# Graph message passing on one core: four groups of three edge tiles in place of six pairs, and normalisation written back into the gather buffer

## What is computed

```python
h = jnp.maximum(_layernorm(x, axis=-1), 0.0)
x_i, x_j = h[src], h[dst]
x_ij = jnp.concatenate([x_i, x_j], axis=1)
m_ij = jax.nn.relu(x_ij @ W.T + b)
out = jax.ops.segment_sum(m_ij, src, num_segments=50000)
return x + out
```

## Time and profile before

| | |
|---|---|
| median of three runs | 763.47 us (762.25 to 765.0) |
| the profiled execution | 760.78 us, span 759.1 us |
| TensorE | 717.7 us busy, 95% of the span |
| VectorE | 590.6 us, 78% |
| ScalarE | 470.0 us, 62% |
| GpSimd | 365.3 us, 48% |
| mean DMA rate | 241 GB/s |

### The profile page before, as it was taken

One profiled execution on the slowest core, in us unless ns is written; L12 is line 12 of the kernel. 1 busy time (PEld: TensorE's weight loads), 2 busy tenths in 40 slices (PEclk: granted clock), 3 DMA queues, 4 the chain that ended last, 5 costly groups with the idle time before them and its releaser, 6 DMA issues.

```text
span 759.1 us, 13504 instructions
## 1 busy us (share of the span) xinstructions
PE 717.7 (95%) x3490; PEld 589.7 (78%) x3490; DVE 590.6 (78%) x1972; ACT 470.0 (62%) x892; POOL 365.3 (48%) x305
## 2 busy tenths in 40 slices
PE   7699999999999999999999999999999999999940
PEld 6578888888888888888888888888888888888830
DVE  4588788788888888878888888878878878878620
ACT  5466667567577576576576576566666666666510
POOL 7632232232232232322167777777776777644433
PEclk9899999999999999999999999999999999999985
DMA  8999999999999999999868787878878787856564
GB/s 276 360 381 365 364 351 374 349 374 362 370 364 359 372 369 351 372 363 344 314 117 142 159 133 147 152 151 133 167 129 152 143 135 143 148 65 78 63 82 55
DMA packets 35750, 182.72 MB, mean 241 GB/s; under 512 B 7306, under 2 KB 7502, under 8 KB 33720
## 3 DMA queue, kind: packets, MB, share of 16 engines
q0 software_dynamic: 29792, 77.00, 49.5%
q1 hardware_dynamic: 5552, 105.39, 36.1%
q10 hardware_dynamic: 392, 0.20, 0.1%
HBM read 156.96 MB, written 128.61 MB: 376 GB/s over the span
## 4 chain that ended last, share of the span: by engine, by line
PE 78%; DMA 9%; issue 5%; POOL 5%; DVE 1%; ACT 0%; SPq 0%; POOLq 0%; DVEq 0%; ACTq 0%
PE z_ps L514 20%; PE z_ps L515 20%; PE z_ps L516 20%; PE ht_ps L498 10%; DMA out<-ring,add_i 6%; POOL out L203 4%; DMA xg<-x,dst_i 3%; POOL xg L187 2%; PE agg_ps L526 1%; PE agg_ps L532 1%; PE agg_ps L527 1%; PE agg_ps L528 1%; PE agg_ps L531 1%; PE agg_ps L529 1%; DMA src_i<-src_cols 0%
## 5 line engine op out<-in xcount | busy, mean ns | idle before, releaser
L514 PE MATMUL z_ps<-w_hi,ht_hi 128*128 128x512 f32 x784 | 319.2, 407 | 1.9 <-DVE w_lo L355 1.1
L515 PE MATMUL z_ps<-w_lo,ht_hi 128*128 128x512 f32 x784 | 310.5, 396 | 0.0
L516 PE MATMUL z_ps<-w_hi,ht_lo 128*128 128x512 f32 x784 | 310.3, 396 | 0.0
L398 ACT CAST ht_hi<-ht_ps 128x512 fp32r<-128x512 f32 x196 | 105.9, 590 | 231.8 <-PE ht_ps L498 231.5
L187 POOL DMA_INDIRECT xg<-x,src_i x98 | 103.1, 1052 | 237.8 <-ACT h L407 223.0
L203 POOL DMA_INDIRECT out<-ring,add_i x98 | 157.7, 1609 | 117.9 <-DMA out<-ring,add_i 82.4
L516 PEld LDWEIGHTS z_ps<-w_hi,ht_lo 128*128 128x128 f32 x784 | 147.6, 188 | 36.0
L514 PEld LDWEIGHTS z_ps<-w_hi,ht_hi 128*128 128x128 f32 x784 | 147.9, 189 | 34.0 <-issue 1.5
L515 PEld LDWEIGHTS z_ps<-w_lo,ht_hi 128*128 128x128 f32 x784 | 148.1, 189 | 31.8
L241 DVE BATCH_NORM_STATS2 stats<-xg 128x6 f32<-128x512 f32 x196 | 125.6, 682 | 15.7 <-DMA xg<-x,dst_i 11.0
L414 ACT ACTIVATE h<-h,rstd 128x512 f32<-128x512 f32 x196 | 131.7, 727 | 2.3 <-DVE rstd L268 2.3
(11 more groups left out here) (45 smaller groups left out, 434.1 us busy)
## 6 DMA issues: line engine op xcount, KB each, us to landing
out<-x SPq DMA_DIRECT2D x125, 800.0 KB, 8.5
ring<-w_t SPq DMA_DIRECT2D x4, 512.0 KB, 4.6
xg<-x,src_i POOLq DMA_INDIRECT x98, 9.5
xg<-x,dst_i POOLq DMA_INDIRECT x98, 23.8
out<-ring,add_i POOLq DMA_INDIRECT x98, 5.0
row_lanes<-src_rows ACTq DMA_DIRECT2D x49, 4.0 KB
out<-x SPq DMA_DIRECT2D x1, 512.0 KB, 9.0
bias_bc<-bias SPq DMA_DIRECT2D x1, 256.0 KB, 8.1
```

The source lines that it names most:

```text
L398: nc.scalar.copy(ht_hi[:, b, s, :], ht_ps[b][s][:, :]).then_inc(hi_ready, 1)
L514: nc.tensor.matmul(z_ps[b][:, :], hi, w_hi[:, c, :], start=(c == 0), stop=False)
L515: nc.tensor.matmul(z_ps[b][:, :], hi, w_lo[:, c, :], start=False, stop=False)
L516: last = nc.tensor.matmul(z_ps[b][:, :], lo, w_hi[:, c, :], start=False, stop=(c == K - 1))
```

## The change

Tiles 0 to 83 stay in 42 pairs. Tiles 84 to 95 form four groups of three in place of six pairs, and tiles 96 and 97 stay a pair. In a group of three the comparison has up to 384 columns, and the first tile's sum has six matmuls, the second's four and the third's two. There are still two accumulators for sums, so the third sum uses the first one's again: it is made one step later, after the first has been stored. ScalarE stores the first two sums at the start of its step and the third after `centre`. The spare region has 384 rows in place of 256, and SyncE fills one that much larger. Each group waits for the group before it to land.

Both passes of the normalisation write into the slot of `xg` that they read, and `h` is gone. So TensorE's transposes read the slot, and the gather of tile t waits for them (`transposed`) and no longer for `centred`. ScalarE's `centre` loses its wait for `transposed`. TensorE's loop has eight steps in its body in place of two, since the slot is named in the instruction, and the last steps are written out from tile 83 on.

```diff
+    TRIPLES = 4
+    FIRST3 = TILES - 2 - 3 * TRIPLES
+    GROUPS = ([(f, 2) for f in range(0, FIRST3, 2)] + [(f, 3) for f in range(FIRST3, TILES - 2, 3)]
+              + [(TILES - 2, 2)])
...
             def gather(t):
                 b = t % XS
                 if t >= XS:
-                    pool.wait_ge(centred, SIDES * (t - XS + 1))
+                    pool.wait_ge(transposed, SIDES * (t - XS + 1))
...
-            def add(pair):
+            def add(group):
+                first, size = GROUPS[group]
...
-                    pool.wait_ge(scattered, 32 * pair)
-                pool.wait_ge(add_ready, 2 * pair + 2)
-                for t in (2 * pair, 2 * pair + 1):
+                    pool.wait_ge(scattered, 16 * first)
+                pool.wait_ge(add_ready, first + size)
+                for t in range(first, first + size):
...
-            sp.dma_start(out[N:N + 2 * P, :], x[0:2 * P, :]).then_inc(spare_filled, 16)
+            sp.dma_start(out[N:N + 3 * P, :], x[0:3 * P, :]).then_inc(spare_filled, 16)
...
-                if not (isinstance(t, int) and t < 2):
-                    act.wait_ge(transposed, SIDES * (t - 1))
                 for s in range(SIDES):
-                    nc.scalar.activation(h[:, b, s, :], xg[:, m, s, :], ACT.Relu, bias=neg_mean[:, b, s:s + 1]
+                    nc.scalar.activation(xg[:, m, s, :], xg[:, m, s, :], ACT.Relu, bias=neg_mean[:, b, s:s + 1]
...
-                    nc.scalar.activation(h[:, b, s, :], h[:, b, s, :], ACT.Copy, scale=rstd[:, b, s:s + 1]
+                    nc.scalar.activation(xg[:, m, s, :], xg[:, m, s, :], ACT.Copy, scale=rstd[:, b, s:s + 1]
...
+            def first_sums_of_triple(t):
+                pe.wait_ge(same_ready, t + 3)
+                pe.wait_ge(ring_filled, t)
+                pe.wait_ge(mlo_ready, t + 3)
+                sum_of(0, ((0, 0), (1, 1), (3, 2)))
+                sum_of(1, ((2, 1), (4, 2)))
+            def last_sum_of_triple(t):
+                pe.wait_ge(ring_filled, t + 1)
+                sum_of(0, ((5, 2),))
...
-            with pe.Fori(3, TILES - 4, 2) as s:
-                for d in range(2):
-                    step(s + d, (3 + d) % 2)
+            with pe.Fori(3, 3 + XS * (rounds - 1) + 1, XS) as s:
+                for d in range(XS):
+                    step(s + d, (3 + d) % XS, pair=d % 2 == 1)
```

More of the change, by code:

```diff
@@ L141, in gnn_message_passing_kernel, with place, sums_before @@
         ring_filled = sem("ring_filled")
+        def place(t, b):
+            if not isinstance(t, int) or t < FIRST3 or t >= TILES - 2:
+                return b, t - b, 2
+            pos = (t - FIRST3) % 3
+            return pos, t - pos, 3
+        def sums_before(t, b):
+            pos, first, size = place(t, b)
+            if isinstance(t, int) and first == 0:
+                return 0
+            last = place(first - 1, 1)[2] if isinstance(t, int) else 2
+            return first - last + min(pos + 1, last)
         block = ctx.enter_context(nc.Block())
@@ L225, in _ @@
             for t in range(FIRST_ADD, TILES):
-                while added < min((t - FIRST_ADD + 1) * 7 // 8, (t - 7) // 2):
+                while added < (t - FIRST_ADD + 1) * 7 // 8 and sum(GROUPS[added]) <= t - 7:
                     add(added)
@@ L229, in _ @@
                 gather(t)
-            for pair in range(added, PAIRS):
-                add(pair)
+            for group in range(added, len(GROUPS)):
+                add(group)
             pool.wait_ge(scattered, 16 * TILES)
@@ L432, in store_sums @@
                 for b in range(2):
-                    act.wait_ge(agg_done, t + b + 1)
-                    slot = t + b - RING if again else t + b
-                    nc.scalar.copy(ring[:, bass.ds(slot, 1), :].rearrange("p a o -> p (a o)"), agg_ps[b][:, :]
-                                   ).then_inc(ring_filled, 1)
+                    store_sum(t + b, b, again)
             def step(s, m, again=False):
@@ L450, in step @@
                     centre(s + 2, (m + 2) % XS)
-                if b and has(-3):
-                    store_sums(s - 3, again)
+                if triple:
+                    store_sum(s - 2, 0, True)
+                if b and has(-3) and place(s - 3, 0)[2] == 2:
+                    store_pair(s - 3, again)
                 if b and has(-3) and has(2 * ROWS - 2):
@@ L491, in _, with transposes @@
         def _(pe):
-            def transposes(t, b):
+            def transposes(t, m):
+                b = m % 2
                 for s in range(SIDES):
@@ L517, in products, with sum_of, sums_of_pair @@
                 last.then_inc(mm_done, 1)
-            def sums(t):
+            def sum_of(bank, terms):
+                for n, (blk, pos) in enumerate(terms):
+                    nc.tensor.matmul(agg_ps[bank][:, :], same[:, blk, :], m_hi[:, pos, :], start=(n == 0), stop=False)
+                    last = nc.tensor.matmul(agg_ps[bank][:, :], same[:, blk, :], m_lo[:, pos, :], start=False,
+                                            stop=(n == len(terms) - 1))
+                last.then_inc(agg_done, 1)
+            def sums_of_pair(t):
                 pe.wait_ge(same_ready, t + 2)
@@ L539, in step @@
                 if has(1):
-                    transposes(s + 1, 1 - b)
+                    transposes(s + 1, (m + 1) % XS)
+                if rest:
+                    last_sum_of_triple(s - 4)
                 if has(0):
                     products(s, b)
-                if not b and has(-2):
-                    sums(s - 2)
+                if pair:
+                    sums_of_pair(s - 2)
+                if triple:
+                    first_sums_of_triple(s - 3)
             pe.wait_ge(consts, 4)
```

128 lines of the change are left out of this document (77 added, 51 removed).

## The result

The changed kernel takes 757.08 us (median of 22 runs), the kernel before 761.67 us (median of 22, the three of the forecast among them). The ratio is 0.9938, with a 95% interval of 0.992 to 0.9956. The forecast was 759.3 against 763.47, a ratio of 0.9945. So the time moved by the size forecast. The profile shows that one term of the sum was there and another was not.

The account below looks back on a forecast made before the run. GpSimd's queue of scatter-adds was taken as the bound: 759.1 - 6.5 (groups) + 3.7 (gathers' wait) = 756.3 us span, 758.0 with what lies around it. Forecast 759.3 us, the middle of 758.0 and 760.7; range 755.8 to 763.8.

Parts of the forecast that it names:

- What bounds the kernel: From 380.89 us GpSimd's queue of adds, each pair waiting for landings, sets the end; TensorE has about 15 us to spare.
- The groups of three, 6.5 us: Tiles 84 to 95 on GpSimd: four groups at 9.56 us replace six pairs at 7.45, saving 6.5 us.
- the rival in which it gains nothing: Third add on GpSimd waits, a group takes 11.2 us, only the gathers' cost is left: 767.2 us; chance 0.10.
- The gathers' wait, 3.7 us: Gathers of tiles 96 and 97 wait for TensorE's transposes of tiles 88 and 89, delaying later adds by 3.7 us.
- the gate: The gather of tile t may start only once tile t-8 is transposed; priced at 3.7 us, bounds 0 to 5.3.
- The middle between two medians: Unsure where 2.7 us between profiled run and median lie, it took 759.3 us, between 758.0 and 760.7.
- no cost at the gate: Rival: adds late by 3.7 us or more, or TensorE ahead, keep the whole 6.5 us: 757.0 us; chance 0.15.
- TensorE's added work: Sums of the groups need 48 matmuls against 36, 2.8 us more, last sums stored at 735.0, covered by 10 us.
- The loop: Rival: TensorE's eight-step loop stalls at its branch, nine jumps at 0.4 us, 3.6 us: 762.9 us; chance 0.10.
- Late gathers in the copy phase: Rival: gathers issued later during the copy (tiles 17, 18) land late and delay TensorE 1 to 3 us: 761.3; chance 0.15.
- The spare region: 128 more rows copied before the first add, 0.7 us, at most twice that; hidden under the gathers' wait, counted as nothing.

Follow-up runs that it names:

- e9: The changed kernel with eight groups of three in place of four, run beside six and ten on one chip; 0.9896 of the kernel before.
- e11: The changed kernel with TensorE's opening dummy transposes raised from 60 to 180; 1.0042 of the kernel before.
- e8: The changed kernel with ten groups of three in place of four; 0.9862 of the kernel before.
- e6: The changed kernel with the third add of each group waiting until the first two have landed; 1.0088 of the kernel before.
- a0: The changed kernel without any edit, run again on another chip; 0.9915 of the kernel before.
- e1: The changed kernel without groups of three, all 98 tiles in pairs; 1.0008 of the kernel before.
- e10: The changed kernel with six groups of three in place of four, run beside eight and ten on one chip; 0.9905 of the kernel before.
- e2: The kernel before with TensorE's loop of eight steps in place of two, nothing else; 1.0005 of the kernel before.
- e7: The kernel before with a spare region of 384 rows filled in place of 256, nothing else; 1.0001 of the kernel before.
- e4: The changed kernel with eight groups of three in place of four, first run of that number; 0.989 of the kernel before.

## Why the prediction was right, and which step of it was not

- **What bounds the kernel.** Right. The queue of adds from 380 us on sets the end in the changed kernel's profile; where TensorE is late its transposes hold up that queue (e9 to e11), and in e8 the sums do so at the very end. e6 shows that one wait more per group costs 13 us with all other work unchanged. The page's own chain seems to say otherwise, since it gives TensorE 80% of the changed kernel's span. It leaves GpSimd at this pair, of tiles 66 and 67, for these two sums:

```profile
635.80 1.62 POOL L221 DMA_INDIRECT out<-ring,add_i  x1 [1.22 <-ACT ring L467]
```

```profile
491.51 1.07 ACT L467 COPY ring<-agg_ps 128x512 f32 x2
```

The sums had been in the ring for 143 us, and the pairs around this one waited 1.1 to 1.3 us for a landing. So this wait too was for a landing, and the chain goes on along GpSimd.
- **The groups of three, 6.5 us.** Right: 6.1 in the profile and 6.3 in a0, at 9.67 and 9.46 us a group where 9.56 was forecast. The third add in flight saves what was forecast, and the rival in which it gains nothing is out.
- **The gathers' wait, 3.7 us, "worked out instruction by instruction".** This is the step that failed, by its certainty. The mechanism is there, and e9 has it at the forecast's two gathers with 3.2 and 2.6 us. But in the changed kernel's profile, a0 and e1 it costs nothing. I set TensorE's times of one execution against GpSimd's times of the same execution, as if the distance between them were a property of the kernel. It is not. TensorE's comes from its start, from how the first gathers land in these two profiles (0.5 or 6.4 us of waiting at tile 3) and from the 13.5 us at its opening in e8 to e10. GpSimd's comes from when the copy ends. The distance between the two goes from 124.8 to 144.7 us in the table. The working also left out that the sums of tiles 84 and 85 move behind the transposes of tile 88, 1.4 us in the gate's favour at one gather, and 0.9 against it at the other.
- **The middle between two medians.** Choosing the middle between 758.0 and 760.7 gave a right ratio, and that was luck in part: it charged some 2.3 us for the gate, where the profile shows none, and the time itself was 2.2 us lower than the 759.3 forecast, as the kernel before was 1.8 us lower in 22 runs than in three. That lateness of the adds can hide the gate is what the table shows. The rival "no cost at the gate", given 0.15, describes the profile of the changed kernel and a0. The median gain, 4.6 us on the first chip, lies between that and the forecast, as it should if some executions pay; that this is the reason there is inferred from profiles elsewhere, not seen in those 22 runs.
- **TensorE's added work.** Right: 12 matmuls, covered. Its last sum is stored from 730.61, before the forecast 735.0, since TensorE was early. ScalarE and VectorE held nothing up.
- **The loop.** No gaps: TensorE is busy all of the time from 60 to 700 us in the changed kernel's profile, and e2 is within 0.3% of nothing. The Trainium skill (Runtime: NRT & Kernel Launch, Instruction fetch mechanics) gives TensorE's store as 128 KiB for 2048 instructions, 64 bytes each, by which the body is an estimated 37 KB. Fetched again on each of the loop's ten turns it would be 0.37 MB, where all instruction transfers of both queues have 0.22 MB. So the trace agrees with the Trainium skill's 128 KiB for TensorE, and not with its line on two blocks of 16 KiB.
- **Late gathers in the copy phase.** VectorE's waits for gathers are 3.7 us in all in the changed kernel's profile, 11.0 before, and 15 to 17 in a0 and e1. e2, with the old gate, has 23.7. So they vary with or without the new gate. They are largest in e10 and e11, 24.4 and 26.7 us, spread over the whole copy phase, both with the new gate and a late TensorE, and both in executions well above their median. e8 and e9 have the same gate and as late a start, and wait at most 1.2 us for gathers. Whether the later issue of gathers has a part in the first two is not shown.
- **The spare region.** Nothing that shows in e7, within 2 us.

What stays open: what decides, execution by execution, how long the first gathers take beside the copy; what holds up TensorE's first transposes in e8 to e10; why the landings of e4's stretch took 3 us more in all, with no wait at the gate; and what the new gate costs beyond the old one when TensorE is late.

## What to carry to other kernels

When one queue ends the kernel by waiting for each of its transfers to land, put more into each wait before making anything else faster; it pays until the engine that makes the data no longer keeps ahead, which with a TensorE 13.5 us late is reached at ten groups. When a change swaps one release for a later one, its price is the distance between two engines. Take that distance from several executions, or give it as a range that starts at zero, and see whether the change itself moves work past the release.

## What the runs showed that was not expected

TensorE at 95% busy had 12 matmuls added to it, and 30 in e8, and the kernel became faster. TensorE's opening is not free either: tripling the dummy transposes, with a mean granted clock of 0.98 as before, cost the whole gain of the change and 0.4% more. Nor does one kernel start alike everywhere: with eight groups TensorE's first product came at 15.0 us on one chip and at 28.5 on another. With three scatter-adds of 128 rows in flight the last lands 5.4 to 5.6 us after its start, with two 5.0 to 5.5, so a third costs a few tenths of a microsecond of landing beside its 1.86 us of GpSimd.
